# Preparing the second block's ternary weights inside the last feed-forward of the first block

## The reference

```
x = x + 0.5 * FFN0(layernorm(x))        # two layers: local attention, then gated (GELU) feed-forward
x = x + linear_attention(layernorm(x))
x = x + 0.5 * FFN0(layernorm(x))        # the same two layers again
x = x + 0.5 * FFN1(layernorm(x))        # ternary feed-forward
x = x + gated_attention(layernorm(x))
x = x + 0.5 * FFN1(layernorm(x))        # the same ternary feed-forward
```

```
quantize(W): gamma = mean(|W|);  clip(round(W / (gamma + 1e-5)), -1, 1)
FFN1(x)    = relu(x @ quantize(W1).T + b1) @ quantize(W2).T + b2     # W1 1024x256, W2 256x1024
```

## Time and profile before

| | |
|---|---|
| median of three runs | 3393.0 us |
| the profiled execution, its own time | 3395.1 us |
| its span in the profile | 3393.3 us |
| mean granted TensorE clock | 0.972 |
| busy: PE, DVE, ACT, POOL | 3124.1, 2379.6, 1678.2, 1468.9 us |

### The profile page before, as it was taken

How to read it: one execution, slowest core, us unless ns; L and a number is a source line. 1 busy time by engine, 2 the same in 40 slices (tenths; PEclk the granted TensorE clock), 3 DMA queues, 4 the chain that set the end, 5 groups by cost and what they waited for, 6 DMA issues and landing times.

```text
span 3393.3 us, 97350 instructions
## 1 busy us (share of the span) xinstructions
PE 3124.1 (92%) x34660; PEld 2706.9 (80%) x34660; DVE 2379.6 (70%) x6688; ACT 1678.2 (49%) x4415; POOL 1468.9 (43%) x1504
## 2 busy tenths in 40 slices
PE   6999999899998989997999989999999994967789
PEld 4888888788887878885888878878887884956678
DVE  6888677777776757675677767777776766755566
ACT  4667732377764225453677742267775222522235
POOL 6777620377772013333777730177774000122320
PEclk9999999999999989998999999999999997988989
DMA  4111121111111110001111121021112101000001
GB/s 150 41 43 44 41 71 34 49 40 38 38 40 49 30 55 7 10 10 46 35 37 38 35 78 34 25 62 38 38 36 66 31 22 30 0 1 0 0 8 43
DMA packets 187170, 126.78 MB, mean 37 GB/s; under 512 B 27756, under 2 KB 183752, under 8 KB 186440
## 3 DMA queue, kind: packets, MB, share of 16 engines
q1 hardware_dynamic: 186952, 123.87, 13.2%
HBM read 48.29 MB, written 25.17 MB: 22 GB/s over the span
## 4 chain that ended last, share of the span: by engine, by line
PE 79%; issue 10%; DVE 4%; POOL 3%; ACT 1%; DMA 1%; SPq 0%; DVEq 0%; POOLq 0%; ACTq 0%
PE bank L291 14%; PE bank L292 11%; PE bank L293 11%; PE bank L444 7%; PE bank L413 6%; PE bank L385 3%; PE bank L585 2%; PE bank L584 2%; PE bank L621 2%; PE bank L622 2%; PE bank L422 2%; PE bank L629 2%; PE bank L628 2%; PE bank L627 2%; PE bank L423 2%
## 5 line engine op out<-in xcount | busy, mean ns | idle before, releaser
L2322 POOL TENSOR_TENSOR prob<-prob,rsum 128x384 f32<-128x384 f32 x512 | 416.0, 834 | 156.4 <-DVE rsum L1564 156.4
L1037 ACT ACTIVATE prob<-prob,nmax 128x192 f32<-128x192 f32 x1024 | 456.2, 454 | 2.3 <-DVE nmax L1557 2.3
L1206 ACT ACTIVATE gate<-bank,bias 128x512 f32<-128x512 f32 x192 | 132.4, 690 | 543.6 <-PE bank L293 543.5
L2309 POOL TENSOR_TENSOR rn<-ss,mhalf 128x16 f32<-128x16 f32 x128 | 375.7, 2935 | 10.7 <-POOL ss L2307 0.2
L2290 POOL TENSOR_TENSOR rstd<-meanvar,eps 128x4 f32<-128x4 f32 x48 | 13.6, 283 | 825.4 <-DVE meanvar L1491 737.8
L291 PE MATMUL bank<-wqkv_hi,hT_hi 128*128 128x512 f32 x768 | 330.3, 430 | 16.0 <-DVE rot_t L1519 8.1
L1557 DVE CUSTOM_DVE_ANT_0 prob<-bank,masks,rn 128x192 f32<-128x192 f32 x768 | 274.5, 414 | 99.3 <-PE bank L413 98.2
L2316 POOL TENSOR_TENSOR qk<-rot_t 128x512 f32<-128x512 f32 x256 | 333.3, 1303 | 6.9 <-DVE ss L1531 6.8
L293 PE MATMUL bank<-wqkv_hi,hT_lo 128*128 128x512 f32 x768 | 304.0, 396 | 0.0
L292 PE MATMUL bank<-wqkv_lo,hT_hi 128*128 128x512 f32 x768 | 304.0, 396 | 0.0
L291 PE MATMUL bank<-gT_hi,w_hi 128*128 128x512 f32 x704 | 276.6, 393 | 2.6 <-issue 2.5
(11 more groups left out here) (274 smaller groups left out, 9556.5 us busy)
## 6 DMA issues: line engine op xcount, KB each, us to landing
Vlo<-V SPq DMA_DIRECT2D x256, 64.0 KB, 2.0
Vhi<-V SPq DMA_DIRECT2D x256, 64.0 KB, 2.0
ya<-Y SPq DMA_DIRECT2D x40, 256.0 KB, 2.3
H<-Y SPq DMA_DIRECT2D x128, 64.0 KB, 1.8
H<-ya SPq DMA_DIRECT2D x128, 64.0 KB, 1.8
yb<-Y SPq DMA_DIRECT2D x128, 64.0 KB, 1.6
HB<-Y SPq DMA_DIRECT2D x32, 256.0 KB, 2.8
HB<-yb SPq DMA_DIRECT2D x32, 256.0 KB, 3.0
```

The costliest lines, as they stand in the source:

```text
L1037: ins = e.activation(pb, pb, ACT.Exp, bias=nm[r][:, x:x + 1], scale=-1.0, accum_out=sums[r][:, x:x + 1])
L2309: e.tensor_tensor(rn[u][:, :], ss[:, :], mhalf[:, :], ALU.pow).then_inc(s_plRN, 1)
L2322: e.tensor_tensor(pair, pair, rs[:, 2 * gi:2 * gi + 2].unsqueeze(2).to_broadcast([P, 2, KW]), ALU.mult).then_inc(s_plPN[gi], 1)
```

## The change

It concerns the end of pass 3, the start of pass 4 and where some tiles lie. The merge and the ternary preparation are cut in pieces and put into the groups of pass 3:

- Sums of absolute values on ScalarE (`size`, two activations of 2048 columns in group 0, which write into the dead table `rot`), thresholds for both weights together after piece 5 of group 0, bias rows behind it on VectorE.
- One eighth of both weights per group on GpSimd (`cut`): four comparisons and two differences of 256 columns into `tern`, from group 1 on; the eighth `cut` follows the last group.
- Behind it on GpSimd the merge of the group before (`merge`: Y times 0.5, then X plus Y, 1024 columns each).
- Four transposes ahead of piece 5 (`turn`, into bank 5) and two copies on ScalarE (`turned`), which write over the eighth of `raw` and `raw2` that was cut.
- Pass 4's first statistics, rows, transposes and splits stand in group 7 of pass 3 (`follow`), and TensorE has pass 4's first piece ahead of pass 3's last second-weight product. No wait for all engines is left between the passes.
- Pass 3's stores to `ya` are gone, since nothing reads them. The gate's weights go to tiles of their own and its rows into `rot`; they are loaded when pass 3's last product is done. The splits of the gate's weights are two instructions instead of one on ScalarE and on VectorE.
- The second ternary product reads W2 as two blocks of 128 columns that lie 1024 apart.

The core of the diff (the sides of the other engines count only):

```diff
@@ tensor
+                    if joined and isinstance(n, int) and n == 0:
+                        if c == 0:
+                            e.wait_ge(s_prepA, cnt['A'] + 2 + CF - 1 + OFF)
+                        if c == 1:
+                            e.wait_ge(s_dvHD, cb + OFF)
+                        if c == CF - 1:
+                            e.wait_ge(s_prepA, cnt['A'] + 2 + CF + OFF)
...
-                            e.matmul(o, hidh[:, c % RING, lt], w2_h[:, c, :], start=False, stop=False, skip_group_check=True)
+                            e.matmul(o, hidh[:, c % RING, lt], raw2_r[:, :, c * P:(c + 1) * P], start=False, stop=False, skip_group_check=True)
...
+                def thresholds():
+                    e.wait_ge(s_prepA, cnt['A'] + 2 + OFF)
+                    e.wait_ge(s_prepB, cnt['B'] + 1 + OFF)
+                    e.matmul(bank[5][:, 0:2], ones[:, :], thr[:, 0:2], start=True, stop=True).then_inc(s_prepP, 1)
+
+                def turn(j, o):
+                    e.wait_ge(s_prepB, cnt['B'] + 2 * j + 4 + OFF)
+                    for i in range(4):
+                        x = e.transpose(o[:, i * P:(i + 1) * P], tern[:, i * P:(i + 1) * P], identf)
+                    x.then_inc(s_prepP, 1)
...
                     for c in range(nch):
+                        if ternary and c == CH - 1 and not first:
+                            e.wait_ge(s_dvHD, cb + nch * n + c - 1 + OFF)
+                            turn(n - 1, bank[5])
                         piece(n, c, par)
+                        if ternary and c == CH - 1 and first:
+                            thresholds()
+                        if pending and c == 0:
+                            pending()
+                        if pending and c == 2:
+                            turn(CF - 1, bank[3])
                         if c == TRAT and not final_:
                             tr(n + 1)
+                        if c == TRAT and final_ and follow:
+                            follow()
@@ scalar
+                def size(W, i):
+                    e.activation(rot[:, :, :, :].rearrange('p a t d -> p (a t d)'), W, ACT.Abs, accum_out=thr[:, i:i + 1]).then_inc(s_prepA, 1)
+
+                def turned(j, x):
+                    e.wait_ge(s_prepP, cnt['P'] + 2 + j + OFF)
+                    e.activation(raw_r[:, bass.ds(D * j, D)], x[:, 0:D], ACT.Copy)
+                    e.activation(raw2_r[:, :, bass.ds(P * j, P)], x[:, D:2 * D].rearrange('p (k f) -> p k f', k=KD), ACT.Copy).then_inc(s_prepA, 1)
@@ vector
-            merge()
-            prep_F()
             loads_gate()
-            ffn(NRUN, CH * GRP * NRUN, False)
+            first_norm[3](finish)
...
+                        if follow and not more:
+                            if c == 0:
+                                follow[0]()
+                            if c == 2:
+                                follow[1]()
+                            if c == 3:
+                                follow[2]()
@@ gpsimd
+                def cut(j):
+                    e.wait_ge(s_prepV, cnt['V'] + 3 + OFF)
+                    e.wait_ge(s_prepP, cnt['P'] + 1 + j + OFF)
+                    a_, b_ = (raw[:, bass.ds(D * j, D)], W2raw[:, :, bass.ds(P * j, P)])
+
+                    e.tensor_scalar(tern[:, 0:D], a_, thr[:, 6:7], None, ALU.is_lt)
+                    e.tensor_scalar(tern2, b_, thr[:, 7:8], None, ALU.is_lt)
+                    e.tensor_scalar(a_, a_, thr[:, 4:5], None, ALU.is_gt)
+                    e.tensor_scalar(b_, b_, thr[:, 5:6], None, ALU.is_gt).then_inc(s_prepB, 1)
+                    e.wait_ge(s_prepB, cnt['B'] + 2 * j + 3 + OFF)
+                    e.tensor_tensor(tern[:, 0:D], a_, tern[:, 0:D], ALU.subtract)
+                    e.tensor_tensor(tern2, b_, tern2, ALU.subtract).then_inc(s_prepB, 1)
+
+                def merge(n):
+                    e.wait_ge(s_dvYB, U * (G0 + n + 1) + OFF)
+                    v, w = (X[:, bass.ds(U * n, U), :], Y[:, bass.ds(U * n, U), :])
+                    e.tensor_scalar(flat(w), flat(w), 0.5, None, ALU.mult).then_inc(s_mdvY, 1)
+                    e.wait_ge(s_mdvY, 2 * n + 1 + OFF)
+                    e.tensor_tensor(flat(v), flat(v), flat(w), ALU.add).then_inc(s_mdvY, 1)
+
                 def group(n, last):
                     if not last:
                         ffn_stats(pas, l0, n + 1)
+                    elif ternary:
+                        ffn_stats(NRUN, False, 0)
+                    if ternary and not (isinstance(n, int) and n == 0):
+                        cut(n - 1)
+                        merge(n - 1)
```

More of the change, by code:

```diff
@@ L536, in loads_F, with ffn @@
                 prep['raw2'] += 16
-            def prep_F():
-                Wa, Wb = (raw[:, 0:CF * D], raw2[:, 0:2048])
                 prep['small'] += 32
[L541 to L564, removed]
+                cnt.update(prep)
+                prep['A'] += 2 + CF
+                prep['P'] += 1 + CF
+                prep['V'] += 5
+                prep['B'] += 2 + 2 * CF
+            last_w2 = []
+            def ffn(pas, cb, l0, final=False, next_loads=None, more=False, follow=None):
+                ternary, joined = l0 and pas == NRUN - 1, pas == NRUN
                 nch, LAG, TRAT = (CH, 2, 3) if l0 else (CF, 3, 5)
@@ L1176, in tr @@
                     G = G0 + n
+                    behind = ternary and isinstance(n, int) and n == GRP
                     e.wait_ge(s_peG, cb + nch * (n - 1) + OFF)
@@ L1229, in ffn @@
                 group(GRP - 1, 1)
-                if not more:
+                if not more and not ternary:
                     e.wait_ge(s_dvYB, U * (G0 + GRP) + OFF)
-            def merge():
-                e.wait_ge(s_mdvY, GRP + OFF)
             def loads_lin():
@@ L1749, in ffn @@
-            def ffn(pas, cb, l0, final=False, next_loads=None, more=False):
+                cnt.update(prep)
+                prep['A'] += 2 + CF
+                prep['P'] += 1 + CF
+                prep['V'] += 5
+                prep['B'] += 2 + 2 * CF
+            def ffn(pas, cb, l0, final=False, next_loads=None, more=False, follow=None):
+                ternary = l0 and pas == NRUN - 1
                 nch = CH if l0 else CF
@@ L1834, in gated_group @@
                     for c in range(CH):
+                        if ternary and first and c == CH - 1:
+                            thresholds()
                         gated_piece(n, c)
@@ L1876, in rest @@
                         next_loads()
-                    group(0, 0)
+                    if pending:
+                        relu_group(0, 0, pending)
+                    else:
+                        group(0, 0)
                     loop(GRP // 2 - 1, lambda i: (group(2 * i + 1, 1), group(2 * i + 2, 0)))
                     group(GRP - 1, 1)
-                    if not more:
+                    if not more and not ternary:
                         finish()
@@ L2441, in ffn @@
                     rotary_tables()
-                loop(GRP - 2, lambda i: group(i + 1, False))
+                if ternary:
+                    for n in range(1, GRP - 1):
+                        group(n, False)
+                else:
+                    loop(GRP - 2, lambda i: group(i + 1, False))
                 group(GRP - 1, True)
-                if not more:
+                if ternary:
+                    cut(CF - 1)
+                    merge(GRP - 1)
+                elif not more:
                     e.wait_ge(s_dvYB, U * (G0 + GRP) + OFF)
-            def merge():
-                e.wait_ge(s_mdvY, GRP + OFF)
             def loads_lin():
```

326 lines of the change are left out of this document (123 added, 203 removed).

## The result

The changed kernel takes 3358.1 us (median of four runs, 3357.9 to 3361.2) against 3392.7 (four runs of the kernel before): a ratio of 0.9899, with a 95% interval of 0.9882 to 0.9916. That is 34.5 us faster.

A forecast was written before the change was run, and what follows sets the result against it. TensorE bounds the kernel, so gains come where it stands, between passes 3 and 4. -54.1 + 4.3 + 26.6 + 3 + 0.3 = -19.9 us; from the median of 3393.0, forecast 3373, range 3348 to 3391.

The forecast's parts named there:

- What goes: Between pass 3 and pass 4: TensorE's gap of 52.4 us and 1.7 us of low clock after it vanish, 54.1 us.
- What TensorE gets: On TensorE's path: eight transposes 0.8, eight turns 3.2 and the thresholds' matmul 0.3 add 4.3 us.
- Hidden work: In pass 3's groups: ScalarE, VectorE and GpSimd additions hidden; GpSimd 7.4 us more a group, a comparison priced 0.5 us.
- the walk: Group 1, instruction by instruction: VectorE and GpSimd take turns, Xn comes late and TensorE waits 4.0 us.
- The price of running together: Groups 1 to 7 of pass 3: GpSimd holding VectorE delays Xn, 3.8 us a group, 26.6 us in all.
- The Trainium skill's rule: VectorE and GpSimd hold a port pair by exclusive lock; by that the four Xn rows are blocked, not merely slowed.
- The seam: Between pass 3 and pass 4: VectorE's last addition and GpSimd's last merge make pass 4's rows late, 3 us (0 to 5).
- The gate's splits and the two-block operand: Splits as two instructions on the path cost 0.3 us; W2 read as two blocks in the ternary second product costs nothing.
- rival A: Pass 3's groups: alternation of VectorE and GpSimd costs little, 0 to 2.2 us a group, 3346 to 3362; chance 0.22.

The follow-up runs named there:

- the kernel without waits: Changed kernel with GpSimd's group merges and differences waiting for the fourth Xn, and the seam's inverse root ahead of the last merge: 3347.3 us, ratio 0.9863.
- The product with two inputs: Changed kernel with the merge's product as a TENSOR_TENSOR with a tile of ones instead of a TENSOR_SCALAR with a constant: 3392.8 us.
- merge on VectorE: Changed kernel with the merge as one VectorE instruction per group, GpSimd keeping only the cuts: 3350.2 us.

## Why the prediction was right and wrong

- **What goes, 54.1 us.** Right, as far as the sum of it and the next term shows. With all waits moved away the stretch is 275.9 - 226.8 = 49.1 us shorter, and 54.1 - 4.3 less the last wait of 1.05 is 48.8.
- **What TensorE gets, 4.3 us.** Right: a turn delays the next matmul by 0.35 (2649.71 to 2650.06), and the period without waits is 24.54 against 24.12, so 0.4 a turn as forecast.
- **Hidden work.** Right for ScalarE, VectorE's thresholds and the turns: no wait of TensorE's names them. The prices on GpSimd were wrong by a factor of two. The step was "I go by the row that it is nearest to: one input, 256 columns, the copy". The copy's 0.40 us was the wrong neighbour; a comparison takes 0.92 to 1.02 us, more than the 0.75 of a two-input instruction. It had cover to spare, so the error cost nothing by itself. By the walk it should have cost much: for a comparison of 1.0 us it gives 7.9 us a group.
- **The price of running together, 26.6 us.** This is the step that failed. The walk let comparisons and the product hold VectorE for their whole length, as the sums and differences do. The case that came out is nearly the one it named in half a sentence, "if the GpSimd operations with one tile input don't hold VectorE, 0 to 2.2". Seven groups lost 7.9 us: the period of the changed kernel is 25.67 on average (2643.17 to 2797.18 in six periods), 1.13 more than the 24.54 of the kernel without waits. The two halves of the walk were each wrong, in opposite directions: the comparison twice as long, and its hold nearly nothing. The product with two inputs shows that the turns themselves were read rightly, one VectorE instruction for one of GpSimd's. The mistake was to take the 1440 ns of the earlier trace rows as proof for all GpSimd instructions. All six of L1453's long executions in the trace of before (from 68.00 to 313.45) stand beside a TENSOR_TENSOR of 512 columns that takes 1.28 to 1.38 us, the five of 1.44 us among them. The one-input ones of that trace (copies of 0.40 us, TENSOR_SCALARs of 16 columns) stand beside VectorE instructions that read a bank, reduce or take statistics, and these keep their usual lengths; none stands beside a CAST, an Xn or a low part that reads SBUF alone.
- **The Trainium skill's rule.** "SBUF — State Buffer", section "Who interferes with whom", has the lock held for the whole GpSimd instruction. The two-input instructions agree (2.77 us beside 2.45, 5.94 for four Xn beside 2.41 and 2.34). The one-input product doesn't: two Xn run at their usual 0.40 us inside its 2.78, and only its beginning and its end hold VectorE.
- **The seam, 3 us.** The place and the cause were right, the size was half: 3.87 us of waiting and 2.4 of low clock. VectorE had Y ready about when it was due (2812.9, 2.6 us after the last product), but the product took 2.78, not 1.4, and the root 2.0, not 1.5; that the clock falls within such a wait and stays low up to 2827 had not been priced in this term, though the earlier trace rows show it for the gap.
- **The gate's splits and the two-block operand.** The splits were put at 0.3 us; TensorE stands for 12.89 us instead of 12.72 ahead of the gated attention's first transposes. The operand costs nothing, as forecast.
- **The whole.** -54.1 + 4.3 + 7.9 + 3.9 + 2.4 = -35.6 us in the stretch, 36.1 measured; the 0.57 us that pass 4's first group waited for Xn in the kernel before are gone too. The forecast's own number was 15 us off: 18.7 us too much for the groups, 3.3 too little for the seam. The time lies in the stated range because that took in rival A.
- **The chances.** 0.22 for A and 0.50 for the forecast were the wrong way round, since nothing in the trace spoke for the one-input case either way and the walk took one end of it for the middle.

## What to carry to other kernels

Work put on GpSimd beside a busy VectorE costs by what it stands next to, and by its kind (TENSOR_TENSOR with two tile inputs, or TENSOR_SCALAR with one), more than by its length: look which GpSimd instructions with two SBUF inputs stand beside the VectorE instruction on which TensorE waits next, and let them wait until it is done; the wait costs nothing if the queue behind has slack. A price read from a neighbour needs both ends carried through the walk, not only through the sum. At a seam, put the short instruction that another engine needs ahead of the long one that nobody needs yet.

## What the runs showed of the hardware

- GpSimd, one tile input: 0.92 us for 256 columns and 2.78 for 1024 of float32, which gives 2.4 ns a column and 0.3 us fixed (two points); two inputs: 0.73 and 2.45. A copy of 256 columns is 0.40. A threshold in a tile costs no more than a constant.
- A GpSimd TENSOR_SCALAR of 2.78 us delays a VectorE TENSOR_SCALAR that stands at its start by 0.7 to 0.8 us, and a CAST that starts 0.8 us before its end by 0.7; between, Xn and low parts keep their usual 0.40 and 0.69. Beside comparisons of 0.92 us, Xn takes 0.53 to 0.58. A GpSimd TENSOR_TENSOR of 256 columns or more delays a VectorE CAST, TENSOR_TENSOR or TENSOR_SCALAR on SBUF to about its own end. Why the first kind lets VectorE pass isn't settled by these runs.
- Not every two-input GpSimd instruction does this: the CAST at 2635.14 takes its usual 0.43 us inside the inverse root of 4 columns and 1.27 us. Nor does every VectorE instruction suffer: beside GpSimd's TENSOR_TENSOR of 512 columns (L2309 of the changed kernel, 1.28 us) the TENSOR_REDUCE from SBUF (L1554) keeps its 0.67 to 0.69 us and the statistics (L1460) their 0.41.
- TensorE's granted clock stayed at 1.00 over waits of 1.05 us in each group and at the seam, and over one of 1.39 (merge on VectorE). Within a wait of 3.87 us it fell to the lower level, eight transposes took 1.97 us instead of 1.09, and it came back at 2827, 5 us behind the wait. With waits of 4.3 us a group it fell at each of the seven.
